# Graph network on one core: where W, xT, x2 and x3 start in on-chip memory, and one matmul of zeros per step instead of two

## The reference

```python
# block 1: one graph layer, divided by the row sums, then residual and norm
h   = x @ W0 + b0
x1  = _layernorm(x + (adj @ h) / adj.sum(-1, keepdims=True))
# block 2: three graph layers, then residual and norm
x2  = relu(adj @ (x1 @ W1) + b1)
x3  = relu(adj @ (x2 @ W2) + b2)
out = adj @ (x3 @ W3) + b3
y   = _layernorm(x1 + out)
```

## The kernel before, in words

| product | what | columns, matmuls | stationary, start | moving, start |
|---|---|---|---|---|
| p5 | adj times s2 of old | 512, 24 | s2, 0 | adj, 0 |
| p2 | adj times x1 of new | 512, 24 | x1, 0 | adj, 0 |
| seam | zeros | 64, 1 | zeros, 64 | zeros, 64 |
| p6 | x3 times W3 of old | 256, 24 | x3, 64 | W, 0 |
| p3 | W1 times g of new | 512, 12 | W, 0 | g, 64 |
| p7 | adj times s3 of old | 256, 48 | adj, 0 | s3, 64 |
| seam | zeros | 64, 1 | zeros, 64 | zeros, 64 |
| p0 | xT times W0 of nxt | 256, 24 | xT, 64 | W, 0 |
| p4 | x2 times W2 of new | 256, 24 | x2, 64 | W, 0 |
| p1 | adj times h of nxt | 256, 48 | adj, 0 | h, 64 |

## Time and profile before

### The profile page before, as it was taken

The page is one execution under the profiler, slowest core; times in us unless marked ns, Lnnn a source line. Parts: engine busy times, 40 slices in busy tenths (PEclk is TensorE's granted clock), DMA queues, the critical chain, the costliest instruction groups (busy, mean ns, idle before and its releaser), DMA issues.

```text
span 549.3 us, 10686 instructions
## 1 busy us (share of the span) xinstructions
PE 537.1 (98%) x3695; PEld 496.8 (90%) x3695; DVE 347.2 (63%) x1032; ACT 306.6 (56%) x757; POOL 209.9 (38%) x225
## 2 busy tenths in 40 slices
PE   6899999999999999999999999999999999999996
PEld 6778998989899898998989899898998989899896
DVE  3874674756657475674756657475674756657546
ACT  4455646566555656656566555656656566554532
POOL 1954409063270814509063270814509063271100
PEclk8999999999999999999999999999999999999999
DMA  8630070511607033070511507033070521500002
GB/s 251 229 153 1 1 269 1 197 74 47 222 0 265 2 101 166 0 267 0 186 81 50 217 0 264 4 109 158 0 267 0 180 89 51 218 2 39 1 1 78
DMA packets 15286, 58.23 MB, mean 106 GB/s; under 512 B 1952, under 2 KB 2720, under 8 KB 13472
## 3 DMA queue, kind: packets, MB, share of 16 engines
q1 hardware_dynamic: 14688, 56.24, 28.4%
q10 hardware_dynamic: 576, 1.70, 0.9%
HBM read 49.55 MB, written 8.39 MB: 105 GB/s over the span
## 4 chain that ended last, share of the span: by engine, by line
PE 93%; DVE 3%; DMA 1%; ACT 1%; issue 1%; POOL 0%; SPq 0%; DVEq 0%; POOLq 0%
PE bank_a L173 16%; PE bank_a L174 16%; PE bank_a L175 16%; PE bank_b L173 15%; PE bank_b L174 15%; PE bank_b L175 15%; DMA xT_raw<-in_xT 1%; POOL adj_lo L867 0%; DVE stats L737 0%; ACT std L558 0%; DVE h_lo L637 0%; DVE xT_lo L637 0%; ACT x_hi L537 0%; DVE moments L749 0%; DVE v L730 0%
## 5 line engine op out<-in xcount | busy, mean ns | idle before, releaser
L846 POOL TENSOR_TENSOR adj_lo<-adj_raw,adj_hi 128x512 fp32r<-128x512 f32 x56 | 70.8, 1295 | 269.0 <-ACT adj_hi L459 269.0
L637 DVE TENSOR_TENSOR x_lo<-bank_a,x_hi 128x512 fp32r<-128x512 f32 x64 | 44.3, 691 | 69.5 <-ACT bank_a L539 69.5
L173 PE MATMUL bank_b<-h_hi,adj_hi 128*128 128x256 f32 (+1 forms) x272 | 75.6, 278 | 2.2 <-DVE h_lo L637 1.9
L175 PE MATMUL bank_b<-h_hi,adj_lo 128*128 128x256 f32 (+1 forms) x272 | 75.4, 277 | 0.0
L174 PE MATMUL bank_b<-h_lo,adj_hi 128*128 128x256 f32 (+1 forms) x272 | 75.4, 277 | 0.0
L514 ACT ACTIVATE std<-moments,eps_col 128x1 f32<-128x1 f32 x64 | 18.9, 295 | 95.5 <-DVE moments L707 95.5
L175 PE MATMUL bank_b<-s_hi,adj_lo 128*128 128x256 f32 x232 | 64.1, 276 | 0.0
L173 PE MATMUL bank_b<-s_hi,adj_hi 128*128 128x256 f32 x232 | 64.0, 276 | 0.0
L174 PE MATMUL bank_b<-s_lo,adj_hi 128*128 128x256 f32 x232 | 64.0, 276 | 0.0
L537 ACT ACTIVATE x_hi<-bank_a,b_col 128x512 fp32r<-128x512 f32 x64 | 43.8, 684 | 23.2 <-PE bank_a L175 22.0
L173 PEld LDWEIGHTS bank_b<-h_hi,adj_hi 128*128 128x128 f32 x272 | 51.1, 188 | 2.6 <-DVE h_lo L637 2.1
(11 more groups left out here) (109 smaller groups left out, 1632.1 us busy)
## 6 DMA issues: line engine op xcount, KB each, us to landing
adj_raw<-in_adjT SPq DMA_DIRECT2D x28, 512.0 KB, 5.4
adj_rows<-in_adj SPq DMA_DIRECT2D x14, 1024.0 KB, 9.4
out_y<-y SPq DMA_DIRECT2D x15, 512.0 KB, 2.9
xT_raw<-in_xT SPq DMA_DIRECT2D x14, 512.0 KB, 6.5
x_raw<-in_x SPq DMA_DIRECT2D x14, 512.0 KB, 7.4
w_raw<-in_w SPq DMA_DIRECT2D x4, 256.0 KB, 6.3
adj_raw<-in_adjT ACTq DMA_DIRECT2D x2, 512.0 KB, 6.6
adj_rows<-in_adjT SPq DMA_DIRECT2D x2, 512.0 KB, 5.9
```

Of the source, the lines that this page charges most:

```text
L173: pe.matmul(acc, st[0], mv[0], start=start, stop=False)
L175: return pe.matmul(acc, st[1], mv[0], start=False, stop=stop)
L637: return dve.tensor_tensor(lo, full, hi.bitcast(F32), ALU.subtract)
L846: pool.tensor_tensor(adj_lo[:, s, k, :], raw[:, k, :], adj_hi[:, s, k, :].bitcast(F32), ALU.subtract).then_inc(adj_split, 1)
```

## The change

The calls that give out memory are put in another order, so that the two small arrays stand behind xT, x2 and x3 and ahead of W. W now starts at 64, and xT, x2 and x3 at 0; adj, x1 and s2 stay at 0, and g, s3 and h at 64. The seam of p0 goes. Nothing else is changed: no other instruction, size or wait.

```diff
-        w_hi, w_lo = pair("w", [P, 4, KF, F])
         adj_hi, adj_lo = pair("adj", [P, RING, T, N])
         x1_hi, x1_lo = pair("x1", [P, T, F])
         s2_hi, s2_lo = pair("s2", [P, T, F])
+        xT_hi, xT_lo = pair("xT", [P, T, F])
+        x2_hi, x2_lo = pair("x2", [P, KF, N])
+        x3_hi, x3_lo = pair("x3", [P, KF, N])
 
 
         inv_rows = sb("inv_rows", [P, T], F32)
         std1 = sb("std1", [P, T], F32)
 
-        xT_hi, xT_lo = pair("xT", [P, T, F])
+        w_hi, w_lo = pair("w", [P, 4, KF, F])
         g_hi, g_lo = pair("g", [P, KF, N])
-        x2_hi, x2_lo = pair("x2", [P, KF, N])
-        x3_hi, x3_lo = pair("x3", [P, KF, N])
         s3_hi, s3_lo = pair("s3", [P, T, F])
         h_hi, h_lo = pair("h", [P, T, H_ROW])
...
                     if reader is not None:
 
                         pe.wait_ge(reader, at(read, T, j + 1))
-                        if j == 0:
-                            seam(banks[0])
 
                 xw_product(p0_done, banks, (features(xT_hi), features(xT_lo)), 0, ready)
```

## The result

The changed kernel takes 560.13 us in the median of four runs (559.78 to 560.65), before it was 551.28 in the same runs: a ratio of 1.0163, 95% interval 1.0147 to 1.0180. It is slower, where 549.1 us was forecast, and outside the range, which ended at 558.6. Rival B had 559.9 us. Times here are medians of executions at a mean granted clock of 0.99 or more; left out is one execution, of an earlier run with 128 bytes of padding ahead of W, that had a granted clock of 0.56 and took 903.13 us (the other one of that run took 559.39 us).

What follows compares the result with a forecast made beforehand. TensorE, busy throughout the steps, was taken as the bound, time being the distances between matmul starts. 551.15 - 2.1 (p0's seam) - 0.1 (last p4) = 548.95, median 0.12 above: 549.1 us; range 548.4 to 558.6.

Steps and rivals of the forecast that it cites:

- Rival B: Steps: rival A, and p6's matmuls unsettled (117.8 ns) too, +1.6 us more, 559.9 us; chance 0.05.
- What bounds the kernel, and the two rates: Steps: only distances between matmul starts make the time; 256 columns take 113.3 ns (settled) or 117.8 ns (unsettled).
- p0's seam, 0.15 us per step: Ahead of p0, 14 times: removing the seam saves its 0.03 us and the stretched distances behind it, 2.1 us.
- p6 keeps its seam: Seam into p6, 15 times, now leading to (0, 64) instead of (64, 0): no change; bounds +1.6 and -0.15 us.
- p7, p4, p1 ... 0: Products p7, p4, p1 (also p5, p2) in the steps: p4 gets p1's and p7's settled pair; change 0.
- rival A: From p3 to p7: settled rate lost until p5, 144 matmuls x 4.5 ns per step, 558.3 us; chance 0.21.
- p3: 512-column product, 15 times, going from (0, 64) to (64, 64): change 0, bounds +0.45 and -0.45 us.
- The last p4, -0.1: Last step's p4, now following p7 with the same pair: settled, 24 x 4.5 ns = 0.1 us off.
- Rival D: p0's stretched first matmul belongs to the operand switch, not the seam: only 14 x 0.03 us back, 550.8 us; chance 0.05.

Runs made afterwards that it cites:

- the kernel with starts chosen product by product: Against the kernel before: W split, W1, W3, xT, x2 at 0, W0, W2, x3 at 64, only p6's seam; 549.11 us, ratio 0.9962.
- The run with W1 at 64: The kernel with starts chosen product by product, but W1 moved from the array at 0 to the one at 64; 557.57 us, 1.0115.

## Why the prediction was wrong

- *What bounds the kernel, and the two rates:* right. Nothing but the distances between matmuls changed, and they took the two values read from before, 113.3 and 117.8 ns.
- *p0's seam, 0.15 us per step:* right in itself, as the kernel with starts chosen product by product shows (2.72 us for p0, 549.11 us in all, the forecast's time). In the changed kernel there was nothing settled left to keep, and taking p0's seam away still saved 0.11 us per step against the same layout with it (2.94 to 2.83 us for p0).
- *"p6 keeps its seam ... I take no change: the seam did the same for two different predecessors":* this is the first step that failed. Both places had the same successor, (64, 0). I varied in thought what the trace varied, the predecessor, and took the successor for free. It cost 0.10 us per step.
- *"p7, p4, p1 ... 0", and rival A given 0.21:* the second. The trace of before had one product of 512 columns with equal starts that led without a seam into one of 256 with unequal ones, and it was unsettled; I weighed against it that the moving operand does not change from p3 to p7. The run with W1 at 64 shows that this does not help. It was priced at 144 matmuls and 4.5 ns, +0.65 us per step; p7, p0, p4 and p1 take 16.96 us with W1 at 64 and 16.32 with W1 at 0, +0.64.
- *p3:* +0.04 us in the changed kernel (2.79), where 0 was taken and +0.03 was the bound; with p6 settled it was -0.01. The pair (64, 64) of 512 columns reaches 226.7 ns from the fourth matmul on where p6 is settled, and only from the eleventh of its twelve in the changed kernel, where p6 is not.
- *The last p4, -0.1:* wrong, it stayed unsettled with its p7 (117.7 ns).
- *Rival D* falls: p0 followed p7 without a stretched matmul. *Rival B,* given 0.05, is what happened: A and p6 together, 559.9 against 560.13 us. A and B should not have been apart and so thin, since nothing in the rows made p6's entry safe.

The Trainium skill, "TensorE: Matmul & The Clock Gate", section "Step-by-step: what each phase is for", says that loading the next weights takes no read bandwidth from the running matmul. By that sentence alone the starts would be worth nothing, and in the run of TensorE alone they are not: 24 matmuls take 2.72, 2.83 or 2.88 us by the starts of the two operands and by what went ahead. The measurement decides on the time; whether it is the loads that take something from the matmul's reads, no run shows. The Trainium skill, "SBUF — State Buffer", section "Who interferes with whom", says "PE and ACT never wait on anyone": towards the other engines the runs agree, since the rates of 113.3 and 117.8 ns are the same with those engines at work and without them.

What stays open: what inside TensorE makes the two rates. That it is a clash of the two reading streams, of weights and moving columns, in lines of 128 or 256 bytes fits the runs and is not shown by any.

## What to carry to other kernels

Where TensorE runs without a break, look at the distances between the starts of matmuls, product by product: a few ns each, at full clock and with nothing awaited, can be the start addresses of the two operands. Such a rate is inherited from what ran before, so a layout has to be judged as a path through the whole step, and a device that repairs the rate has to be tested with the very successor it gets. Give operands their starts one by one where a shared one forces a bad transition: here splitting W in two arrays turned +1.6% into -0.4%.

## What the runs showed of the hardware

- At 2.4 GHz a matmul of 256 fp32r columns in a row of such takes 113.3, 117.8 or 120.0 ns, and one of 512 takes 226.7, 228.8 or 233.3, by the operands' starts and the history; with TensorE alone as with all engines. Rates in between occur where hi and lo arrays start differently modulo 256, or starts differ by 128.
- The distance between the hi and the lo array counts too: with 4,224 bytes instead of 4,096 no product ran below 116.6 ns in its second half, and (0, 0) of 512 columns went from 226.7 to some 230 (one execution each).
- Whether a seam settles the next product depends on its starts modulo 256 bytes against that product's, and, with arrays 8,192 bytes apart, not on its length from 16 to 256 columns. It costs one turn of a weight load, 0.12 us, however short it is; in the changed kernel it costs that and settles nothing.
